# Reordering a 16-block state recurrence on one core: state stages in halves, a fixed PSUM bank per product, two activation table sets, masked R and all of the solve's copies on ScalarE

## The reference

```
sa = s @ a_t;  s = s * w_t + sa * b_t + v_t * k_t;  y_t = s @ q_t
```

## Time and profile before

| quantity | us |
|---|---|
| median of 3 runs (lowest to highest) | 1238.91 (1236.44 to 1255.37) |
| the profiled execution's own time | 1239.54 |
| its span, first to last instruction | 1237.5 |
| PE busy | 1046.2 (85%) |
| PE weight loads busy | 866.3 (70%) |
| DVE busy | 799.6 (65%) |
| POOL busy | 723.6 (58%) |
| ACT busy | 623.3 (50%) |
| mean granted TensorE clock | 0.871 of full speed |

### The profile page before, as it was taken

The page is one execution under the profiler, slowest core; times in us unless marked ns, Lnnn a source line. Parts: engine busy times, 40 slices in busy tenths (PEclk is TensorE's granted clock), DMA queues, the critical chain, the costliest instruction groups (busy, mean ns, idle before and its releaser), DMA issues.

```text
span 1237.5 us, 42142 instructions
## 1 busy us (share of the span) xinstructions
PE 1046.2 (85%) x16578; PEld 866.3 (70%) x16579; DVE 799.6 (65%) x1752; ACT 623.3 (50%) x1213; POOL 723.6 (58%) x1138
## 2 busy tenths in 40 slices
PE   3668889899898898898999988775469999999995
PEld 2446767777777776777777776563258988888885
DVE  2576686786687686866867758311536666666663
ACT  1464486695776775865847758443102222222221
POOL 1086868977978988888669788680012333333331
PEclk9678898898798898987968969876559999999998
DMA  3113033142142241340422412319334544445440
GB/s 91 18 27 79 11 79 87 17 92 71 29 96 52 48 96 22 78 95 12 87 66 33 96 20 70 84 39 300 130 116 158 169 165 170 168 165 174 161 143 6
DMA packets 208623, 111.98 MB, mean 90 GB/s; under 512 B 172364, under 2 KB 191952, under 8 KB 208080
## 3 DMA queue, kind: packets, MB, share of 16 engines
q1 hardware_dynamic: 204720, 101.29, 30.1%
q0 software_dynamic: 3744, 8.40, 2.0%
HBM read 85.41 MB, written 26.08 MB: 90 GB/s over the span
## 4 chain that ended last, share of the span: by engine, by line
PE 60%; ACT 14%; DVE 11%; issue 10%; DMA 3%; SPq 1%; DVEq 1%; POOL 0%; ACTq 0%; POOLq 0%
PE bank L530 11%; PE bank L823 11%; PE bank L836 7%; PE bank L605 7%; PE ry L636 5%; PE ry L836 4%; PE bank L613 3%; ACT arena L877 2%; PE ry L642 2%; PE bank L658 2%; PE bank L674 2%; PE ry L685 2%; PE bank L558 1%; ACT L963 1%; PE bank L570 1%
## 5 line engine op out<-in xcount | busy, mean ns | idle before, releaser
L1675 POOL TENSOR_TENSOR arena<-arena 128x30 f32<-128x30 f32 (+14 forms) x480 | 336.4, 701 | 37.6
L530 PE MATMUL bank<-arena 128*128 128x256 f32 (+2 forms) x992 | 281.5, 427 | 36.0 <-DMA arena<-in_centT 14.4
L1672 POOL TENSOR_TENSOR arena<-arena 128x30 f32<-128x30 f32 (+14 forms) x480 | 286.0, 596 | 36.4
L530 PEld LDWEIGHTS bank<-arena 128*128 128x128 f32 x992 | 184.9, 207 | 87.7 <-issue 34.4
L823 PEld LDWEIGHTS bank<-arena 128*128 128x128 f32 x1248 | 147.0, 194 | 5.2 <-DVE arena L1571 2.6
L823 PE MATMUL bank<-arena 128*128 128x128 f32 x1248 | 148.2, 278 | 2.0 <-DVE arena L1571 2.0
L1315 DVE TENSOR_TENSOR arena<-bank,arena 128x512 f32<-128x512 f32 x128 | 80.6, 680 | 56.9 <-PE bank L605 56.9
L605 PEld LDWEIGHTS bank<-arena 32*128 32x128 f32 x2048 | 91.4, 264 | 36.2 <-issue 36.0
L605 PE MATMUL bank<-arena 32*128 32x64 f32 x2048 | 97.3, 355 | 17.8 <-DVE arena L1293 12.8
L613 PE MATMUL bank<-arena 128*128 128x128 f32 x576 | 91.1, 299 | 15.1 <-ACT arena L1040 7.4
L613 PEld LDWEIGHTS bank<-arena 128*128 128x128 f32 x576 | 72.3, 153 | 39.5 <-issue 19.7
(11 more groups left out here) (164 smaller groups left out, 1882.2 us busy)
## 6 DMA issues: line engine op xcount, KB each, us to landing
arena<-in_W SPq DMA_DIRECT2D x47, 1024.0 KB, 4.9
scr_n<-arena SPq DMA_DIRECT2D x64, 128.0 KB, 2.6
arena<-scr_n SPq DMA_DIRECT2D x16, 512.0 KB, 3.5
scr_u<-arena SPq DMA_DIRECT2D x16, 512.0 KB, 2.7
arena<-scr_u SPq DMA_DIRECT2D x64, 128.0 KB, 2.8
arena<-in_xTp SPq DMA_DIRECT2D x32, 132.0 KB, 4.1
arena<-in_x SPq DMA_DIRECT2D x64, 64.0 KB, 2.9
scr_x<-arena SPq DMA_DIRECT2D x64, 64.0 KB, 2.0
```

The lines of the kernel that those rows point to most:

```text
L530: mm = pe.matmul(ring.tile(m, name)[0:rows, to], lhsT, rhs, start=(i == 0), stop=(i == len(terms) - 1))
L1672: inv_ok.inc(f"m{s}", TT(t, U[:, 0:s, s:s + 1].broadcast_to(shape), U[:, s:s + 1, s + 1:TB].broadcast_to(shape), ALU.mult))
L1675: inv_ok.inc(f"a{s}", TT(U[:, 0:s, s + 1:TB], U[:, 0:s, s + 1:TB], t, ALU.add))
```

## The change

- **Halves.** `read_state`, `update` and `read_out` take a channel half f. `read_state(n, 0)` closes PE's body n, and `read_state(n-1, 1)` stands near the head of the next one. `update` and `read_out` alternate with `gate_1` between them.
- **Fixed banks.** Each product has one bank for good, written after an `@`. The order of use is checked bank by bank, no longer for all products together.
- **Tables.** ACT's body asks for the set with ln and exp, then the one with sigmoid (and tanh), then ln and exp, then sigmoid: four calls, made in every body from -2 to 18.
- **ScalarE.** `keep_r` is four ACT copies of 128 x 256 scaled by the head mask; the copies of the odd batches are ACT's too.
- **Operands in PSUM.** sigma(z), ma, mk, the log and inverse of the norms, the log variance and its inverse root are written back into their bank, and r is read from its bank; eight DVE operations (`scan`, `t`, `f`, `e2`, `kkn`, `rk`, `q`, `n`) that read two SBUF operands read one from PSUM. `keep_reads` goes.
- **Order.** v, the bonus product and the turned values are made one body earlier (for n+1), `low_1` one body earlier (for n+2), the token log and inverse root one body later. SP issues the token loads after the inverse's transfers. The wait for the weights stands before the first products that use them.

The diff, cut to its core (the four `body` lists stand above in their new order):

```diff
+for n in BODIES:
+    for ahead, names in jobs:
+        for job, bank in (entry.split("@") for entry in names.split()):
+            if self.takes(n + ahead, job):
+                self.open(n + ahead, job, int(bank))
...
-    def bank(self, m, name):
-return self.order[self.place[m, name]][0]
...
     def tile(self, m, name):
-return self.banks[self.bank(m, name)]
+return self.banks[self.home[name]]
...
-chain_pe = Stage(sem("chain_pe"), [(-1, "Y"), (0, "R")])
-chain_dve = Stage(sem("chain_dve"), [(-1, "x0o x1o"), (0, "rme rmo")])
+chain_pe = Stage(sem("chain_pe"), [(-1, "R Y")])
+chain_dve = Stage(sem("chain_dve"), [])
...
-chain_act = Stage(sem("chain_act"), [(-1, "rt0 rt1 x0e x1e ye yo")])
+chain_act = Stage(sem("chain_act"), [(-1, "rm00 rm01 rm10 rm11 rt1 rt0 x0e x0o x1e x1o ye yo")])
...
-         "z": [(proj, s) for s in ("z0", "z1", "abs0", "abs1", "sg0", "sg1")],
...
+         "z": [(comb, "scan")],
...
+         "r": [(comb, "rk"), (comb, "q")], "v": [(proj, "v"), (proj, "vm1")], "kk": [(comb, "kk")], "ss": [(comb, "kkn")],
...
-ring = Ring(banks, [(1, "lo1"), (0, "bk01"), (-2, "var"), (-1, "rt1"), (1, "lo2_1 lo2_2 lo2_0 lo2_3"),
-                    (-3, "xT"), (0, "v"), (-3, "logit"), (1, "h k"), (-2, "g"), (1, "ma mk z a kk"),
-                    (0, "rk"), (-2, "wo"), (-1, "x0"), (1, "ss r"), (-1, "x1"), (1, "tg"),
-                    (0, "bk00 v1 bk10 bk11"), (-1, "su"), (0, "v0"), (1, "sc00 sc01 sc02 sc03"), (-1, "yc"),
-                    (1, "sc10 sc11 sc12 sc13"), (0, "rt0")], filled, freed)
+ring = Ring(banks, [(1, "lo2_1@5 lo2_2@1 lo2_0@3 lo2_3@0"), (-2, "var@4"), (-3, "xT@2"), (1, "k@1"),
+                    (-1, "rt1@5"), (1, "h@2"), (0, "bk10@3"), (-3, "logit@1"), (-1, "rt0@4"),
+                    (1, "z@1 a@2 kk@0"), (-2, "g@5"), (1, "ma@3 mk@0"), (-2, "wo@5"), (-1, "x0@2"),
+                    (1, "ss@4"), (-1, "x1@1"), (1, "r@5"), (0, "bk01@3 bk11@0"), (1, "v@4"), (0, "bk00@0"),
+                    (-1, "su@5"), (1, "tg@2 sc00@0 sc01@3 sc02@2 sc03@1 v1@5 rk@4"), (2, "lo1@1"),
+                    (1, "v0@5 sc10@4 sc11@0 sc12@1 sc13@3"), (-1, "yc@2")], filled, freed)
...
+    def weights(m):
+        if m == 0:
+            pe.wait_ge(w_in, 16 * d["_nloads"])
+
...
-    def read_state(m):
+    def read_state(m, f):
         buf = m % 2
...
+        if m and f == 0:
             state_dve.wait(pe, m - 1, "s")
             chain_act.wait(pe, m - 1, "ye", "yo")
...
+        if f == HALF - 1:
+            chain_pe.inc(m, "R", mm)

     def turn_r(m, f):
-        chain_dve.wait(pe, m, "rme", "rmo")
+        chain_act.wait(pe, m, "rm00", "rm01", "rm10", "rm11")
...
-    def x_kept(m):
-        chain_act.wait(pe, m, "x0e", "x1e")
-        chain_dve.wait(pe, m, "x0o", "x1o")
-
-    def update(m):
+    def x_kept(m, f):
+        chain_act.wait(pe, m, f"x{f}e")
+        chain_act.wait(pe, m, f"x{f}o")
+
+    def update(m, f):
         buf = m % 2
-        x_kept(m)
-        turned.wait(pe, m, "bk00", "bk01", "bk10", "bk11")
-        ring.wait_empty(pe, m, "su")
-        for g in range(NB):
+        x_kept(m, f)
+        turned.wait(pe, m, f"bk{f}0", f"bk{f}1")
+        if f == 0:
+            ring.wait_empty(pe, m, "su")
+        for g in range(f * B, (f + 1) * B):
...
+        if f == HALF - 1:
+            ring.fill(m, "su", mm)
...
-            proj.inc(m, f"{step}{h}", A(dst[:, h], bank(m, name, cols=half(h)), func, bias=prm(bias, h)))
+            src = bank(m, name, cols=half(h))
+            proj.inc(m, f"{step}{h}", A(src if dst is None else dst[:, h], src, func, bias=prm(bias, h)))
+
+    def sigmoid_tables():
+        nc.scalar.preload_act_table_set("sigmoid_and_others")
+
+    def log_exp_tables():
+        nc.scalar.preload_act_table_set("natural_log_exp_and_others")
...
-            comb.wait(act, m - 1, "scan", "ls", "e2")
-        ring.wait_full(act, m, "z")
-        for h in range(HALF):
-            proj.inc(m, f"sg{h}", A(L[:, h], bank(m, "z", cols=half(h)), ACT.Sigmoid, bias=prm("decay", h)))
-        for h in range(HALF):
-            proj.inc(m, f"abs{h}", A(t1[:, h], bank(m, "z", cols=half(h)), ACT.Abs, bias=prm("decay", h)))
-        for h in range(HALF):
-            proj.inc(m, f"z{h}", A(zt[:, h], bank(m, "z", cols=half(h)), ACT.Identity, bias=prm("decay", h)))
+            comb.wait(act, m - 1, "ls", "e2")
+        halves(m, "z", "z", zt, ACT.Identity, "decay")
+
+    def sigma_of_z(m):
+        proj.wait(act, m, "z0", "z1")
+        proj.inc(m, "sg", A(bank(m, "z"), flat(zt), ACT.Sigmoid))
+
+    def abs_of_z(m):
+        if m:
+            comb.wait(act, m - 1, "ls")
+        proj.wait(act, m, "z0", "z1")
+        proj.inc(m, "abs", A(flat(t1), flat(zt), ACT.Abs))
...
-        halves(m, "ma", "ma", ma, ACT.Sigmoid, "misc_a")
+        halves(m, "ma", "ma", None, ACT.Sigmoid, "misc_a")
...
-        halves(m, "mk", "mk", mk, ACT.Sigmoid, "misc_k")
+        halves(m, "mk", "mk", None, ACT.Sigmoid, "misc_k")
...
-        ring.wait_full(act, m, "r")
-        proj.inc(m, "r", A(flat(rt), bank(m, "r"), ACT.Copy))
...
-        proj.inc(m, "lnss", A(flat(nrm), bank(m, "ss"), ACT.Ln, bias=tiny))
+        proj.inc(m, "lnss", A(bank(m, "ss"), bank(m, "ss"), ACT.Ln, bias=tiny))
...
-        proj.inc(m, "inv", A(flat(nrm), flat(nrm), ACT.Exp, scale=-0.5))
+        proj.inc(m, "inv", A(bank(m, "ss"), bank(m, "ss"), ACT.Exp, scale=-0.5))
...
+    def keep_r(m):
+        chain_pe.wait(act, m, "R")
+        if m:
+            ring.wait_full(act, m - 1, "rt0", "rt1")
+        for e in range(2):
+            for h in range(2):
+                chain_act.inc(m, f"rm{e}{h}", A(Rm[:, :, 1 - e, h], RY[e][:, :, 0], ACT.Copy, scale=odd_even[:, h:h + 1]))
...
+        post_act.inc(m, "lnv", A(bank(m, "var"), bank(m, "var"), ACT.Ln, bias=gneps))
...
+        post_act.inc(m, "rstd", A(bank(m, "var"), bank(m, "var"), ACT.Exp, scale=-0.5))
...
+        comb.inc(m, "scan", nc.vector.tensor_tensor_scan(flat(L), within, ring.tile(m, "z")[:, :], 0.0, ALU.mult, ALU.add))
...
+        comb.inc(m, "t", STT(out=flat(rkt), in0=ring.tile(m, "ma")[:, :], scalar=1.0, in1=flat(at), op0=ALU.subtract, op1=ALU.mult))
         comb.wait(dve, m, "t")
-        comb.inc(m, "f", TT(flat(ma), flat(ma), flat(rkt), ALU.subtract))
+        comb.inc(m, "f", TT(flat(ma), ring.tile(m, "ma")[:, :], flat(rkt), ALU.subtract))
...
-        comb.inc(m, "e2", STT(out=flat(mk), in0=flat(zt), scalar=-0.5, in1=flat(mk), op0=ALU.add, op1=ALU.mult))
+        comb.inc(m, "e2", STT(out=flat(mk), in0=flat(zt), scalar=-0.5, in1=ring.tile(m, "mk")[:, :],
+                             op0=ALU.add, op1=ALU.mult))
...
-        comb.inc(m, "rk", TT(flat(rkt), flat(rt), flat(kt), ALU.mult))
+        comb.inc(m, "rk", TT(flat(rkt), ring.tile(m, "r")[:, :], flat(kt), ALU.mult))
...
-        comb.inc(m, "q", TT(aq[m % 2][:, :, 1], tt(rt), Wt[:, :, 1:TB + 1], ALU.mult))
+        ring.wait_full(dve, m, "r")
+        proj.wait(dve, m, "W")
+        comb.inc(m, "q", TT(aq[m % 2][:, :, 1], ring.tile(m, "r")[:, :].rearrange("p (g t) -> p g t", g=NB), Wt[:, :, 1:TB + 1],
+                            ALU.mult))
...
-        comb.inc(m, "kkn", STT(out=flat(kk), in0=flat(nrm), scalar=1e12, in1=flat(kk), op0=ALU.min, op1=ALU.mult))
+        comb.inc(m, "kkn", STT(out=flat(kk), in0=ring.tile(m, "ss")[:, :], scalar=1e12, in1=flat(kk), op0=ALU.min, op1=ALU.mult))
...
-    def keep_r(m):
-        chain_pe.wait(dve, m, "R")
-        if m:
-            ring.wait_full(dve, m - 1, "rt0", "rt1")
-        shape = [P, NB // 2, 2, TB]
-        for e, name in enumerate("eo"):
-            chain_dve.inc(m, f"rm{name}", TT(Rm[:, :, 1 - e], RY[e][:, :, 0, None, :].broadcast_to(shape),
-                                             odd_even[:, None, :, None].broadcast_to(shape), ALU.mult))
...
-        post_dve.inc(m, "n", TT(flat(yc), flat(yc), flat(ysq), ALU.mult))
+        post_dve.inc(m, "n", TT(flat(yc), flat(yc), ring.tile(m, "var")[:, :], ALU.mult))
```

341 lines of the change are left out of this document (168 added, 173 removed).

## The result

The changed kernel takes 1168.46 us (median of 4 runs, 1161.26 to 1175.8) against 1239.98 for the one before on the same chip: a ratio of 0.9435, 95% interval 0.9389 to 0.948. On a second chip it gave 0.945 (0.9383 to 0.9517). I had forecast 1204, with 1172 as the lower end, so the gain is about twice what I said, and outside my range.

A forecast was written before the change was run, and what follows sets the result against it. PE in its written order was taken as the bound: 40.4 + 1.6 + 2.1 + 3.0 = 47.1 us a body against 48.9, -25 over fourteen bodies, start -6, end -4, giving 1204 us; range 1172 to 1248 (forecast's own 1180 to 1226).

The forecast's parts named there:

- Clock: PE's time lost at 1.2 GHz in each body: 3.0 us, against 3.3 before; bounds 0 and 6.8.
- Matmuls: PE's matmuls at full clock in each body: 40.4 us, unchanged because none is added or removed.
- Issue: PE's issue holes, nearly all in `read_out` and `update`: 2.1 us a body, against 2.7 before.
- Waits for ACT: PE's waits for other engines: 1.6 us a body instead of 2.5, with 1.2 before `update(n-1,0)`.
- PSUM operands: Operands in banks shorten POOL's block from about 44.5 to some 41 us; worth nothing by itself.
- Fixed banks: New waits on banks whose last holder is read late, at five places: cost 0; 1 us if DVE is 1 us later.
- A switch of tables: A table load on ACT costs 1.3 us, without the skill page's further drain of about 1380 ns.
- A: Rival: clock and holes clear, low clock 1.6 and holes 0.7, body 44.3 us, time 1165; chance 0.15.
- B: Rival: ACT is the new bound, its chain 2.8 us longer a body, time 1240; chance 0.16.
- C: Rival: `scores(0)` to `centre_y` all at 1.2 GHz, +6.8 us a body instead of +3.0, time 1257; chance 0.12.
- D: Rival: the compiler keeps its own loads before ln and exp, +2.6 us a body, time 1240; chance 0.04.
- E: Rival: a table switch costs 1.28 us beyond its load, PE waits 1.3 longer a body, 1222; chance 0.02.

The follow-up runs named there:

- whole_read: The changed kernel with both halves of the state read together at the end of PE's body; 1210.85 us.
- before_spread: The kernel before with `turn_values` moved between `read_out` and `update`, and `centre_y` between the halves of the state read; gains 0.4%.
- burst: The changed kernel with `gate_1` moved ahead of `read_out(0)`, so four runs of small matmuls follow one another; 1177.56 us, ratio 0.9463.
- whole_mid: whole_read with `centre_y` (1.1 us) moved from ahead of the state read to between its halves; 1194.82 us, ratio 0.9619.
- tables: The changed kernel with two more table loads a body in the middle of ACT's chain; ratio 0.9556.
- sbuf_ops: The changed kernel with six of the eight DVE operations reading both operands from SBUF again, where ACT writes them; ratio 0.9538.
- bonus_first: The changed kernel with the bonus product ahead of `scores(0)` instead of behind it; ratio 0.9588.
- after: The changed kernel itself, against the kernel before; 1168.46 us, ratio 0.9435.
- dve_idle: The changed kernel with the two products of `mask_removal` computed twice on DVE ahead of the scores; 1192.46 us, ratio 0.9614.

## Why the prediction was wrong

*Clock.* This step failed. I kept 3.0 us a body for it, "nearest to today's 3.3", and it is 1.2 to 1.5; the clock of 0.95 also left the 0.84 to 0.93 that I had named. My argument was that a low stretch would still open behind `read_out` and `update`, and that the work now lying in it, `scores` first, "loses more for each us at 1.2 GHz". Two things went otherwise. First, `scores`, which I put into the low stretch, left it (281 ns each in place of 352), and so did the first part of the state read (216 in place of 290). This is there in whole_read too (288 and 218), so it comes from the rest of the new order. The single moves point to large or other work between the small matmuls, without settling it: before_spread has 321 and 258, and burst, where `gate_1` no longer parts them, 302 for `scores`. Second, I had not seen that the state read, 256 small matmuls in one run, would be cut by `low_2` and `variance_y`. I counted it only as work that the clock falls on, and whole_read and whole_mid show it as what makes the clock fall on the large products behind it: whole, it costs 2.25 us a body of busy time, and 1.1 us of large work between its halves gives 1.46 of that back. The "judgement" that 4.5 us of it do not feel the clock was also wrong, by the 290 to 216 ns of its first part.

*Matmuls.* 40.4 was 0.4 too much: 40.0 in two bodies at full clock (39.7 in all five). By it the low clock cost 3.7 us a body before, not 3.3.

*Issue.* 2.1 forecast, 30.6/13 = 2.4 measured. I started from 2.7 a body, where all rows of the trace give 40.2/13 = 3.1, with 2.1 and not 2.5 for the other waits. The size was near and the place was not: I looked at `update` alone. The read kept whole has 1.2 us a body more of holes.

*Waits for ACT.* 1.6 forecast, 0.9 measured. The wait of 1.2 ahead of the second group of `update` doesn't exist, so ACT's chain was shorter than my walk by at least that, and tables shows slack in it. (My walk had one reading wrong: six sigmoids in 2.30 us are 0.38 each, not 0.36.)

Sum of the four: 1.8 + 0.4 - 0.3 + 0.7 = 2.6 us a body beyond 47.1, 34 us in thirteen bodies. That is the miss between the profiles, with 2 at the start (8.4, not 6) and the end, where 12.3 less what the fourteenth body had in my sum (1.8) and the 4 leaves 6.5. At the start `low_2` came at 14.65 and not at 13.4, since the four table loads opened at 8.96 and not at 7.8; the rest of the fill and of the end I didn't take apart.

*PSUM operands.* POOL's time a body fell to 34.7 busy; I had said 41 for its block, which is (577.88 - 66.5)/13 = 39.3 on average. sbuf_ops has 41.9 there and up to half of the gain, with the reserve made above. "Worth nothing by itself" is not refuted and not shown; its ratio is 1% higher at the edge of the intervals.

*Fixed banks* at 0: of the five places that I named, one has a wait, `scores(1)` behind u, 1.0 us over the thirteen bodies (L617 behind DVE L1352). A bank that I had not named has 2.2: `low_1` waits until DVE has masked the scores in it (L535 behind L1362). Together that is 0.25 us a body. bonus_first shows a bank held longer, 13.0 us of waits.

*A switch of tables* is 1.3 us here, as the sum had it. In the changed kernel the next operation starts 0.02 us after the load:

```profile
430.99 1.28 ACT L905 ACT_TABLE_LOAD   x1
432.29 0.63 ACT L985 ACTIVATE arena<-arena 128x512 f32<-128x512 f32 x1
```

Two more switches in the chain made ACT 2.4 us busier (450.42 less 419.39, by 13), two loads of 1.28 less small changes, and the body 1.0 longer. The Trainium skill, "ScalarE: Activation LUTs", *What ACT_TABLE_LOAD costs*, has about 1380 ns of drain beside the 1283 ns of each load, an estimate of 5.3 us for two switches from the page's figures. The load's 1283 ns agree with the trace; the drain doesn't show in it, and the measurement decides.

*Rivals.* What came is A, at 0.15, with its words: "alternating work keeps 2.4 GHz". It put 44.3 us on the body (44.45) and 1165 on the time (1168). That it comes so near is partly luck: its clock term was near (1.6, against 1.2 to 1.5), but its other half, the hole filled to 0.7 us, did not happen (2.4), and the smaller waits for ACT, the matmuls and the end made up for it. My case against it, that the 256 small matmuls of `read_out` and `update` stay almost in a row, looked at the wrong 256. B (ACT the new bound) and C (slower by the clock) left no trace; D and E did not occur, since there are four loads a body (26 and 26 in thirteen), as I had said. B's price is 1204 + 39 = 1243, not 1240; no chance hangs on it.

**Where the 78 us come from.** Split read: 49 by the two profiles (3.80 x 13), of which about 29 clock and 20 holes; they are the shortest and the longest of their runs, and the ratios give 43. The rest of the bodies: 8 by the profiles, for all other parts together, since whole_read's body of 48.25 is only 0.63 under that of before. The 8 hide a trade: against before, whole_read saves 35 us on `scores` and the first part of the read and loses nearly all of it in the large products and elsewhere, as its busy time falls by 2.4 us only. Fill: 8, of which 2 the split wait. Drain: 12, whose bodies I did not take apart. The parts are not additive: the split alone in the old order does not gain. It seems to pay because the rest of the change clears its way; this isn't shown, and how much each of the other parts is needed for it stays open.

## What to carry to other kernels

When TensorE is the bound, list the runs of small matmuls in its order and how much large work parts them: swapping two neighbouring steps so that 2.3 us of large products stood inside a run of 256 was worth 3.5% here, with no work removed, though two like moves in the old order did not pay. Count a run both as work the low clock falls on and as what brings it down on the work behind it. And at the end of a pipelined stage, look at what the DMA queue issues ahead of the last small load: here DVE waited 6.0 us for tokens that stood behind eight large loads. Issued one body later, these loads no longer held the tokens up, and 2.0 us of the wait were won before DVE met its next one.

## What the hardware showed that I had not expected

- Holes of 0.8 to 2.2 us without a releaser, in runs where 64 matmuls pass in 0.75 us. They shrink when other work or another wait comes first: 1.13 us more of large product a body took 0.7 us a body off them and cost no time that the ratio shows (0.9375, against the 0.955 that its own length would give), and a wait for DVE of 20.0 us left 1.5 of 11.8 us of them.
- The low clock outlasts what brought it: behind the whole state read it was granted 0.79 over 24 us of mostly large products, which ran at 3.20 in place of 1.97 us.
- The same clock average can go with more holes (whole_mid: 5.0 us idle a body, 0.95) or fewer (after: 3.2, 0.95), and the same order of work with a lower clock when PE waits more (dve_idle: 3.8, 0.93).
- GpSimd was busy 2.6 us a body less (34.7 in place of 37.3) with six operands of VectorE written to and read from PSUM rather than SBUF, with no change to GpSimd's own instructions; by one profile each, and up to 0.9 of it can be the longer body.
